# Issue order in a fused attention and expert layer: matmul pairs in twos, expert products in one piece, clips on GpSimd

## The reference

```
xn  = layernorm(x)
a1  = attention(xn, Wqkv)                    # "plain"; softmax with exp(clip(s - max, -50, 50))
a2  = attention(rope(xn Wq), rope(xn Wk_c Wk), xn Wv_c Wv)   # "rope"
x1  = rmsnorm(xn + a2 Wo) * norm1
sh  = swiglu(x1 W_shared_in) W_shared_out
h   = swiglu(x1 W1_shared)
w   = top 2 of 4 experts in the likelier of 2 groups, softmax weights
rt  = sum over 8 experts of (h W2[e]) * w[e]
out = x + a1 Wout + rmsnorm(x1 + sh + rt) * norm2
```

## Time and profile before

| | us |
|---|---|
| three runs | 2119.31, 2123.36, 2124.22 |
| median | 2123.36 |
| profiled execution | 2125.91 |
| its span, first to last instruction | 2124.1 |
| TensorE busy | 1992.3 |
| VectorE busy | 1772.0 |
| ScalarE busy | 1461.9 |
| GpSimd busy | 926.2 |

### The profile page before, as it was taken

How to read it: one execution, slowest core, us unless ns; L and a number is a source line. 1 busy time by engine, 2 the same in 40 slices (tenths; PEclk the granted TensorE clock), 3 DMA queues, 4 the chain that set the end, 5 groups by cost and what they waited for, 6 DMA issues and landing times.

```text
span 2124.1 us, 44066 instructions
## 1 busy us (share of the span) xinstructions
PE 1992.3 (94%) x10694; PEld 602.5 (28%) x10694; DVE 1772.0 (83%) x3204; ACT 1461.9 (69%) x2993; POOL 926.2 (44%) x1567
## 2 busy tenths in 40 slices
PE   4999899999999999999999999999999999999985
PEld 1222223232322323232232323223232322323232
DVE  3898998888989888898988889898898989898511
ACT  0367677776777777777776767777677777777752
POOL 1332335354363545535353553535345353544334
PEclk9599899999999999999999999999999999999998
DMA  2101010101001010100101010010101101010000
GB/s 92 42 31 50 25 52 29 58 27 55 31 23 56 30 56 26 54 33 26 55 27 57 26 55 31 24 54 29 53 26 42 48 23 55 30 52 21 22 0 15
DMA packets 79168, 81.93 MB, mean 39 GB/s; under 512 B 14717, under 2 KB 66173, under 8 KB 78845
## 3 DMA queue, kind: packets, MB, share of 16 engines
q1 hardware_dynamic: 78984, 80.20, 11.2%
HBM read 11.36 MB, written 4.19 MB: 7 GB/s over the span
## 4 chain that ended last, share of the span: by engine, by line
PE 73%; DVE 10%; issue 6%; ACT 5%; SPq 3%; DMA 1%; POOL 1%; DVEq 0%; ACTq 0%; POOLq 0%
PE score_ps L468 20%; PE o_ps L503 19%; PE side_ps L583 13%; DVE negmax L756 6%; PE side_ps L570 5%; PE side_ps L552 5%; PE shift_ps L483 4%; ACT weights L618 3%; PE side_ps L519 2%; ACT spread L652 2%; PE side_ps L575 2%; PE side_ps L541 1%; SPq L390 1%; SPq L392 1%; PE side_ps L556 1%
## 5 line engine op out<-in xcount | busy, mean ns | idle before, releaser
L618 ACT ACTIVATE weights<-shift_ps 128x512 f32<-128x512 f32 x2048 | 1157.2, 599 | 516.8 <-PE shift_ps L483 480.9
L756 DVE TENSOR_REDUCE negmax<-score_ps 128x1 f32<-128x512 f32 x2048 | 1319.9, 682 | 215.8 <-PE score_ps L468 187.0
L483 PE MATMUL shift_ps<-qt,kt 51*128 51x512 bf16 x2048 | 713.6, 390 | 34.8 <-ACT weights L618 29.8
L468 PE MATMUL score_ps<-kt,qt 48*128 48x512 bf16 x2048 | 701.6, 396 | 42.0 <-DMA kt<-k_parts 20.7
L503 PE MATMUL o_ps<-weights,vt 128*32 128x512 f32 x4096 | 556.2, 616 | 0.2
L468 PEld LDWEIGHTS score_ps<-kt,qt 48*128 48x128 bf16 x2048 | 149.6, 94 | 891.4 <-DVE negmax L756 754.7
L964 POOL TENSOR_SCALAR weights<-weights 128x2048 f32<-128x2048 f32 x128 | 243.7, 1904 | 179.5 <-ACT weights L618 174.5
L583 PE MATMUL side_ps<-w_sb,hidden 128*128 128x512 f32 x512 | 284.6, 646 | 9.3 <-ACT spread L652 9.3
L483 PEld LDWEIGHTS shift_ps<-qt,kt 51*128 51x128 bf16 x2048 | 161.2, 93 | 161.1 <-ACT weights L618 147.3
L764 DVE TENSOR_SCALAR weights<-weights 128x1024 f32<-128x1024 f32 x256 | 186.0, 727 | 0.0
L1024 POOL TENSOR_TENSOR two<-spread 128x256 f32<-128x256 f32 x128 | 93.1, 727 | 170.8 <-ACT spread L652 146.4
(11 more groups left out here) (112 smaller groups left out, 1502.4 us busy)
## 6 DMA issues: line engine op xcount, KB each, us to landing
qt<-q_parts SPq DMA_DIRECT2D x768, 32.0 KB
kt<-k_parts SPq DMA_DIRECT2D x768, 32.0 KB
x_in<-in_x_dram SPq DMA_DIRECT2D x16, 256.0 KB, 2.7
xn_mid<-xn_new SPq DMA_DIRECT2D x16, 256.0 KB, 2.4
xn_old<-xn_mid SPq DMA_DIRECT2D x16, 256.0 KB, 2.4
res_new<-in_x_dram SPq DMA_DIRECT2D x16, 256.0 KB, 2.7
res_old<-res_new SPq DMA_DIRECT2D x16, 256.0 KB, 2.7
out_dram<-out_sb SPq DMA_DIRECT2D x16, 256.0 KB, 2.6
```

The source lines that it names most:

```text
L468: pe.matmul(score_ps[:, score_bank(a, t), :], qt[a][row:row + HROWS, slot, 128 * tile:128 * tile + 128], kt[a][row:row + HROWS, slot, :], ...
L483: pe.matmul(shift_ps[:, t % 2, :], kt[a][row:row + HROWS + MROWS, slot, 128 * tile:128 * tile + 128], qt[a][row:row + HROWS + MROWS, slot, ...
L618: act.activation(weights[:, i % 8, tile, :], shift_ps[:, t % 2, :], ACT.Exp, scale=SCALE).then_inc(weighed, 1)
L756: dve.tensor_reduce(negmax[:, i // 8, tile, i % 8:i % 8 + 1], score_ps[:, score_bank(a, t), :], AX.X, ALU.max, negate=True).then_inc(max_t ...
```

## The change

The order in a quarter stays. The tables move nearly all side jobs to odd quarters, so that two pairs follow each other before the next job; short jobs (transposes, `max_*`) share a quarter with a value call, 512-column jobs take the odd quarters without one. Each expert product, and `shared_out`, is issued in one go. ScalarE's scaled copies come in two halves, one quarter apart. All 16 clips of a sample are whole heads on GpSimd; VectorE has none. GpSimd's odd list is in a new order, and a few fixed quarters on VectorE and ScalarE are set anew. ScalarE's first tanh of a step waits for a sum that reads the shared memory.

```diff
-EVEN = [("x1T", [0]), ("gates", [3]), ("max_rope1", [6]), ("q_rope", [8]), ("qs_rope", [10]), ("k_rope", [11]),
-        ("ks_rope", [15]), ("up0", [16]), ("down0", [19]), ("o_plain1", [20]), ("back_plain", [23]),
-        ("y_plain", [26]), ("up1", [28]), ("down1", [31]), ("up2", [35]), ("max_plain0", [36]),
-        ("down2", [39]), ("up3", [43]), ("down3", [47]), ("o_rope0", [52]), ("v0", [55]), ("v1", [59])]
-ODD = [("xnT", [0]), ("q_plain", [4]), ("max_plain1", [7]), ("k_plain", [10]), ("shared_out", [12, 14]),
-       ("exp0", [16, 18]), ("o_rope1", [20]), ("back_rope", [23]), ("y_rope", [26]), ("exp1", [27, 28]),
-       ("exp2", [29, 31]), ("exp3", [34, 36]), ("max_rope0", [38]), ("exp4", [40, 42]), ("exp5", [44, 46]),
-       ("exp6", [48, 50]), ("o_plain0", [52]), ("exp7", [55, 58])]
+EVEN = [("x1T", [1]), ("q_rope", [3]), ("max_rope1", [5]), ("gates", [7]), ("qs_rope", [11]), ("k_rope", [15]),
+        ("ks_rope", [19]), ("o_plain1", [21]), ("up0", [23]), ("back_plain", [25]), ("down0", [27]),
+        ("y_plain", [31]), ("up1", [35]), ("down1", [39]), ("max_plain0", [41]), ("up2", [43]), ("down2", [47]),
+        ("up3", [51]), ("o_rope0", [53]), ("v0", [55]), ("down3", [59]), ("v1", [61])]
+ODD = [("xnT", [1]), ("q_plain", [7]), ("max_plain1", [9]), ("k_plain", [11]), ("shared_out", [15]),
+       ("exp0", [19]), ("o_rope1", [21]), ("exp1", [23]), ("back_rope", [25]), ("exp2", [27]), ("y_rope", [31]),
+       ("exp3", [35]), ("exp4", [39]), ("max_rope0", [41]), ("exp5", [43]), ("exp6", [47]), ("exp7", [51]),
+       ("o_plain0", [53])]
...
                     if a == PLAIN:
-                        pe.wait_ge(clip_dve, cnt(b, lag, 16, 4 * quad + 4))
-                        pe.wait_ge(clip_pool, cnt(b, lag, 8, 2 * quad + 2))
+                        pe.wait_ge(clip_pool, cnt(b, lag, H, 4 * quad + 4))
...
-                    mm = pe.matmul(to, hidden[:, 2 + part, 128 * tile:128 * tile + 128],
-                                   w2_sb[:, part, 512 * e:512 * e + 512], start=(part == 0), stop=(part == 1))
-                    if part == 1:
-                        mm.then_inc(side_full[at], 1)
+                    for c in range(2):
+                        mm = pe.matmul(to, hidden[:, 2 + c, 128 * tile:128 * tile + 128],
+                                       w2_sb[:, c, 512 * e:512 * e + 512], start=(c == 0), stop=(c == 1))
+                    mm.then_inc(side_full[at], 1)
...
-                    for e in range(4):
+                    for e in (2 * half, 2 * half + 1):
...
+                            else:
+                                need(act, summed, norms_done(b, -1, 0))
...
-                    if t in (1, 2):
-                        clip(b, -1, H - 1, t - 1)
...
-                    if t % 4 in (1, 2) and t > 4 and (t // 4 - 1) % 2:
-                        clip(b, 0, t // 4 - 1, t % 4 - 1)
-                    for job, rest, quarter in (("q_plain", q_rest, 6), ("k_plain", k_rest, 12)):
+                    for job, rest, quarter in (("q_plain", q_rest, 9), ("k_plain", k_rest, 13)):
...
-                    if t == 29 and live(b, -1):
+                    if t == 36 and live(b, -1):
                         mean_square(b, 0, -1)
-                    if t == 40 and live(b, -1):
+                    if t == 46 and live(b, -1):
                         scale(b, x1, x1, 0, -1, x1_done)
...
             def even(b):
+                clip(b + (-1), 15)
```

More of the change, by code:

```diff
@@ L133, in jobs_at @@
 def jobs_at(step, t):
-    return [(name, at.index(t)) for name, at in TABLE[step] if t in at]
+    return [name for name, at in TABLE[step] if t in at]
 def layer_kernel(nc, x, wq, wkcT, wk, wvcT, wvp, wvr, wo, w_up, w_out, w2, w_gate, bias, norms, consts, out):
@@ L507, in value, with side @@
                 mm.then_inc(valued, 1)
-            def side(b, job, part):
+            def side(b, job):
                 lag = LAG[job]
@@ L513, in side @@
                 to, at = bank(job), side_bank(job)
-                if part == 0:
-                    need(pe, side_free[at], side_uses(b, job))
+                need(pe, side_free[at], side_uses(b, job))
                 def turn(src, n=128):
@@ L572, in side @@
                     taken(pe, b, "down3")
-                    for tile in (2 * part, 2 * part + 1):
+                    for tile in range(NT):
                         for c in range(2):
@@ L601, in step @@
                             value(b, unit - 1, (ROPE, PLAIN)[unit], k // 4, k % 4)
-                    for job, part in jobs_at(which, t):
-                        side(b, job, part)
+                    for job in jobs_at(which, t):
+                        side(b, job)
             all_steps(pe, lambda b: step(b, "even"), lambda b: step(b, "odd"), merge_weights)
@@ L642, in copy_side, with weight_experts @@
                     act.activation(dst, bank(job), ACT.Copy).then_inc(free(job), 1)
-            def weight_experts(b, n):
+            def weight_experts(b, n, half):
                 if live(b, -2):
[L647 to L650, removed]
-                    for e in range(4):
+                    if half == 0:
+                        full(act, b, f"exp{n}")
+                        act.wait_ge(route, cnt(b, -2, ROUTE_A + ROUTE_B, ROUTE_A + ROUTE_B))
+                        if n >= 2:
+                            act.wait_ge(mixed, cnt(b, -2, 24, 3 * (n - 2) + 1))
+                    for e in (2 * half, 2 * half + 1):
                         last = act.activation(spread[:, n % 2, e, :], bank(f"exp{n}")[:, 128 * e:128 * e + 128],
                                               ACT.Copy, scale=gate[:, n // 2, 4 * (n % 2) + e:4 * (n % 2) + e + 1])
-                    last.then_inc(free(f"exp{n}"), 1)
+                    if half == 1:
+                        last.then_inc(free(f"exp{n}"), 1)
             def part(b, lag, t, job, quarter, a, src, parts, hi):
@@ L681, in even @@
                         copy_max(b, "max_rope1")
-                    part(b, 0, t, "q_rope", after("even", "qs_rope", 3), ROPE, roped[:, 0, :], q_parts, True)
-                    part(b, 0, t, "k_rope", after("even", "ks_rope", 3), ROPE, roped[:, 1, :], k_parts, True)
+                    part(b, 0, t, "q_rope", after("even", "qs_rope", 5), ROPE, roped[:, 0, :], q_parts, True)
+                    part(b, 0, t, "k_rope", after("even", "ks_rope", 6), ROPE, roped[:, 1, :], k_parts, True)
                     for n in range(4):
@@ L691, in even @@
                         copy_o(b, "o_plain1", "o_plain0", -1)
-                    part(b, 0, t, "q_rope", after("even", "qs_rope", 10), ROPE, q_rest[:, :], q_parts, False)
-                    part(b, 0, t, "k_rope", after("even", "ks_rope", 8), ROPE, k_rest[:, :], k_parts, False)
+                    part(b, 0, t, "q_rope", after("even", "qs_rope", 12), ROPE, q_rest[:, :], q_parts, False)
+                    part(b, 0, t, "k_rope", after("even", "ks_rope", 11), ROPE, k_rest[:, :], k_parts, False)
                     if t == after("even", "back_plain"):
@@ L720, in odd @@
                     for n in range(8):
-                        if t == after("odd", f"exp{n}"):
-                            weight_experts(b, n)
+                        for half in range(2):
+                            if t == after("odd", f"exp{n}", 1 + half):
+                                weight_experts(b, n, half)
                     if t == 18:
@@ L838, in even @@
                         add_side(b, "y_plain", res_new[:], res_new[:])
-                    if t == 44 and live(b, -2):
+                    if t == 42 and live(b, -2):
                         dve.wait_ge(route, cnt(b, -2, ROUTE_A + ROUTE_B, ROUTE_A - 1))
@@ L1085, in odd @@
                 clip(b, 0)
+                clip(b, 1)
                 third(b, 1, PLAIN, 0, q_rest, q_parts)
@@ L1088, in odd @@
                 third(b, 1, PLAIN, 1, k_rest, k_parts)
-                place_v(b, ROPE)
+                clip(b, 3)
                 clip(b, 4)
                 mix(b, 0)
+                clip(b, 5)
+                mix(b, 1)
                 clip(b, 6)
+                mix(b, 2)
+                clip(b, 7)
                 if live(b, -1):
@@ L1095, in odd @@
                     pool.tensor_tensor(square, x1[:], x1[:], ALU.mult).then_inc(squared, 1)
-                    root(b, -1, 0)
-                mix(b, 1)
-                mix(b, 2)
                 split_max(b, "max_rope0")
                 clip(b, 8)
+                if live(b, -1):
+                    root(b, -1, 0)
                 mix(b, 3)
+                place_v(b, ROPE)
+                clip(b, 9)
                 mix(b, 4)
@@ L1104, in odd @@
                 mix(b, 5)
+                clip(b, 11)
                 mix(b, 6)
@@ L1107, in odd @@
                 mix(b, 7)
+                clip(b, 13)
                 clip(b, 14)
```

9 lines of the change are left out of this document (1 added, 8 removed).

## The result

The changed kernel takes 2114.14 us (median of 11 runs, 2107.27 to 2117.57), the kernel before 2124.01 beside it (11 runs, 2116.97 to 2147.45); the ratio is 0.9936, 95% interval 0.9907 to 0.9966. So it is faster by 10 us in the median, where 46 were forecast. The profiled execution took 2110.22, 15.7 less than that of before.

The account below looks back on a forecast made before the run. TensorE was taken to set the pace, with VectorE a close second. Terms summed to -2.45 us a pass, -34 over 14 samples; with -12 for the first samples, 2125.9 became 2080, median 2077, range 2036 to 2120.

Parts of the forecast that it names:

- Fewer excursions: TensorE leaves its score-and-shift pairs for other work 21 times less a pass, at 0.09 to 0.10 each: -2.0 us.
- products in one piece: Expert products and the shared one on TensorE, issued unsplit, take 1.92 us each instead of 2.12: -1.7 a pass.
- Longer runs: Runs of four pairs without another job, in the odd step and across step ends, wait for ScalarE: +2.65 us a pass.
- VectorE without clips: With 16 half clips gone from VectorE, waits behind side work shrink: -2.9 us a pass, bounds -1.0 and -4.5.
- third kind of wait: TensorE's waits behind side work of VectorE or ScalarE: eleven places a pass, 4.5 us in sum, about 1.6 left after.
- GpSimd late at t = 53: The odd step's value call at t = 53 waits for GpSimd's clips of heads 8 to 11: +1.5 us a pass.
- The loop's end: The standstill at the loop's end stays; x1T moved behind the value call gives -0.3 us a pass.
- The first samples: Odd steps of samples 0 and 1, without products and paced by VectorE, lose 6 us each: -12, bounds 0 and -20.
- The clock: Granted-clock falls at loop ends, five of twelve before: all twelve would add 21 us, none give back 15; no chance given.
- Rival 1: GpSimd sets the odd step's pace, later at t = 53: +2.25 us a pass, 2142 in all; chance 0.10.
- rival 2: All waits melt, runs costing no more than now and GpSimd in time: -6.6 us a pass, 2019; chance 0.13.
- rival 3: The even step stays at VectorE's pace, runs cost their upper bound: +0.8 us a pass, 2122, no change; chance 0.13.

Follow-up runs that it names:

- e6: The changed kernel with four runs of four pairs broken by moved jobs, and GpSimd's clip 13 ahead of mix 7: 2096.39 us, ratio 0.9885.
- e2: The changed kernel with every ScalarE copy or tanh that followed an even quarter's exp moved behind an odd one: 2075.63 us, ratio 0.9775.
- e3: The changed kernel with clips of odd heads back on VectorE in two halves each, GpSimd clipping even heads alone: 2170.67 us, ratio 1.021.
- e7: The changed kernel with the edits of e2 and e6 in one, and the first tanh one quarter earlier: 2090.26 us, ratio 0.9839.
- e13: The changed kernel with GpSimd's odd list reordered: v placed behind clip 4, mixes 0 to 2 later, mix 5 behind clip 11: 2153.18 us, ratio 1.0146.
- e4: The kernel before with all sixteen clips as whole heads on GpSimd; tables, products and ScalarE's places as before: 2140.25 us, ratio 1.0079.
- e12: e7 with x1T moved to t = 63 of the odd step and GpSimd's list in the order of e13: 2039.2 us, ratio 0.9608.
- e5: The changed kernel with gates and q_rope exchanged, gates again at t = 3 right behind the loop's end: 2123.28 us, ratio 0.9989.
- e15: e13 with VectorE's four scalings of x1 at t = 54 in place of t = 46: 2172.38 us, ratio 1.0231.

## Why the prediction was wrong, step by step

- **Fewer excursions, products in one piece** (-2.0 and -1.7): right. Bare work fell by 3.6, forecast 3.7; a product takes 1.91 to the next pair (1206.99 to 1208.90), forecast 1.92.
- **Longer runs** (+2.65): right. The four runs inside the steps wait 1.43, 1.43, 0.94 and 1.0, as costed. e6 gave back 3.0 of them.
- **VectorE without clips** (-2.9): this is the step that failed. It has the third kind of wait fall from 4.5 to about 1.6 a pass. That 1.6 came of walking the new tables with VectorE's maxima and side jobs; ScalarE enters only as the one that frees the products' banks, and its side work between two exps has no price. The new tables put nearly every job at an odd t, so ScalarE's part, a quarter later, lands between the two exps of a two: 4.0 a pass, and with the other waits of this kind close to 7 (13.6 less 4.8 in the runs and about 2 at the loop's end). e2 removes those twelve, and 0.5 in each of two runs, and gains 38.5, where 37 were missing. That the two agree is in part luck: its pass is still 0.6 longer than forecast, since other waits, as the one of 1.2 for down0's bank, come up behind those removed, and 10 us of its gain lie ahead of the loop. The clips' move is itself worth about what was forecast in these tables (56 in e3, partly the clock's; forecast 2.9 x 14 + 12 = 53).
- **GpSimd late at t = 53** (+1.5): its lower bound, 0, came true; as far as e7 shows, because TensorE came later than forecast. In e7, where TensorE is early, it is 2.12. The clips did cost something, but on the other engine: VectorE's scalings stand while one runs, 3.32 in place of 2.07, and TensorE waits for them at t = 50. The Trainium skill (SBUF — State Buffer, Who interferes with whom) calls the port pair that VectorE shares with GpSimd an exclusive lock, for which a VectorE instruction with two inputs in SBUF contends with a GpSimd instruction that reads SBUF, and a tensor_reduce on this chip never does. The rows agree with both: e13's scalings take 4.49 beside 3.86 of clips, and the maxima keep their 0.60 (below).
- **The loop's end** (-0.3): more. From the value call's end (990.30) to q_rope (995.17) stand 4.87 with 3.11 of work, so 1.8 of wait where 2.6 was forecast.
- **The first samples** (-12): wrong, -0.4. From first score to first score the odd step of sample 1 fell by 3.3, but that of sample 0 rose by 2.9: value calls of 1.86 there, up to 122 us in place of 112, show TensorE at its lower level for longer (the trace's record of the clock begins only at 123 us). VectorE led that step before, as the prediction had it, but at 35.4 busy of 51 it no longer did, and TensorE took its place.
- **The clock**: "no case of its own", and none of twelve falls was priced at -15 and set aside. It is what happened in the profiled execution, and it is that execution's gain; how much of the median's 10 us it is stays open. There the two errors of size, 15 short here and 12 over in the first samples, nearly cancel, which is luck; ScalarE's places are what is left.
- **Rival 1** has its wait at t = 53 in e4, in the old tables, but 0.58 long; **rival 2** needs all of e12's edits (2039, where it said 2019); **rival 3** came near in time for another reason: the even step did shrink, by 1.0.

Open: what makes the clock fall at some loop ends and not at others (e5), and whether e15 would gain with a gap of GpSimd long enough for the scalings; that wasn't tried.

## What to carry to other kernels

When jobs are regrouped on the engine that sets the pace, walk every engine that serves it at the new places, not only the one that the change relieves: a consumer's side work must come behind the last of the pairs it feeds, not between them. Work moved to an engine with room is judged by its tightest reader, by what stands ahead of it in the in-order list, and by what it stops on a neighbour. And a wait that is taken away uncovers the next: e2 and e6 together lost until GpSimd's order was mended.

## What the runs showed of the hardware

- A long wait of TensorE can cost more than its length: behind 2.12 us (e7, every pass of the loop), 1.77 (e13, seven of twelve) and 2.96 (e15, every pass) the granted clock went to 1.2 GHz, with 0.67 of full speed over the 9.5 us behind e7's, and a product took 3.66 in place of 1.92.
- Four scalings on VectorE take 1.63 beside GpSimd's mix, 3.32 beside one clip of 1.89, and 4.49 beside two. The maxima of the scores, which read PSUM, keep 0.60 each (five in 3.07) beside a mix and the next clip. Half a clip on VectorE, 0.60 otherwise, took 2.12 beside a clip of GpSimd (e3).
